# A grouped convolution moved between two parts of a linear layer's products on TensorE

## What is computed

```python
out = lax.conv_general_dilated(x, weight, ..., feature_group_count=4)   # 32 -> 32 channels, 9 taps
out = out + ctx[:, :, None] + bias[None, :, None]
base_out = einsum('btd,od->bto', out, base_W) + base_b                  # 512 -> 512
logits = einsum('btd,nd->btn', out, router_W) + router_b                # 15 routes
topk_p, topk_i = top_k(softmax(logits), 8)
w = einsum('btk,btke->bte', topk_p, onehot(expert_map[topk_i]))         # weight of each of 8 experts
h = einsum('btd,erd->bter', out, A)                                     # 8 x 16 = 128 columns
lora = einsum('bter,eor->bto', h * w[..., None], B) * 2.0
x + base_out + lora
```

## Time and profile before

| | us |
|---|---|
| median of three runs | 198.47 (196.33 to 198.89) |
| the profiled execution | 197.38 |
| its span, first to last instruction | 195.6 |
| TensorE busy | 187.3 |
| VectorE busy | 161.1 |
| GpSimd busy | 139.1 |

### The profile page before, as it was taken

One profiled execution on the slowest core, in us unless ns is written; L12 is line 12 of the kernel. 1 busy time (PEld: TensorE's weight loads), 2 busy tenths in 40 slices (PEclk: granted clock), 3 DMA queues, 4 the chain that ended last, 5 costly groups with the idle time before them and its releaser, 6 DMA issues.

```text
span 195.6 us, 4329 instructions
## 1 busy us (share of the span) xinstructions
PE 187.3 (96%) x1297; PEld 180.1 (92%) x1297; DVE 161.1 (82%) x547; ACT 76.9 (39%) x197; POOL 139.1 (71%) x115
## 2 busy tenths in 40 slices
PE   7899699999999999999999999999999999998993
PEld 2788599999999999999999999999999999997992
DVE  0899987888889888889888889888898889775663
ACT  3674434434333444433334444343344443122210
POOL 4539796777887777777887777778877777943520
PEclk9999969999999999999999999999999999999999
DMA  5985442455444434445443335444334133333312
GB/s 180 312 292 214 111 140 80 159 167 162 146 124 124 152 116 153 162 162 157 125 140 123 134 130 162 162 162 147 137 110 150 71 86 111 107 107 109 111 54 107
DMA packets 19051, 27.66 MB, mean 141 GB/s; under 512 B 2144, under 2 KB 9696, under 8 KB 19040
## 3 DMA queue, kind: packets, MB, share of 16 engines
q1 hardware_dynamic: 18576, 27.05, 42.6%
q10 hardware_dynamic: 432, 0.48, 0.7%
q0 software_dynamic: 32, 0.01, 0.2%
HBM read 19.14 MB, written 8.39 MB: 141 GB/s over the span
## 4 chain that ended last, share of the span: by engine, by line
PE 83%; DVE 8%; DMA 4%; issue 2%; ACT 1%; DVEq 0%; ACTq 0%
PE wide_ps L516 53%; PE conv_banks L498 15%; PE wide_ps L540 10%; DMA wide_sb<-wide_w 2%; DMA x_in<-x_first 2%; PE hwt_bank L527 2%; PE conv_banks L516 1%; DVE terms L672 1%; DVE y_rows L647 1%; DVE xr L642 1%; DVE wide_lo L757 1%; DVE y L731 1%; DVE spread L703 0%; DVE expert_w L707 0%; ACT wide_hi L324 0%
## 5 line engine op out<-in xcount | busy, mean ns | idle before, releaser
L516 PE MATMUL wide_ps<-wide_hi,y_hi 128*128 128x400 f32 (+1 forms) x248 | 80.4, 329 | 1.1 <-DVE xr L642 0.8
L516 PE MATMUL wide_ps<-wide_lo,y_hi 128*128 128x400 f32 (+1 forms) x248 | 77.1, 315 | 0.0
L516 PE MATMUL wide_ps<-wide_hi,y_lo 128*128 128x400 f32 (+1 forms) x248 | 76.8, 314 | 0.0
L437 POOL TENSOR_TENSOR terms_lo<-terms,terms_hi 128x768 fp32r<-128x768 f32 x28 | 51.6, 1842 | 31.8 <-ACT terms_hi L345 31.8
L516 PEld LDWEIGHTS wide_ps<-wide_hi,y_hi 128*128 128x128 f32 x248 | 46.6, 189 | 3.5 <-issue 1.0
L516 PEld LDWEIGHTS wide_ps<-wide_lo,y_hi 128*128 128x128 f32 x248 | 46.9, 190 | 0.0
L516 PEld LDWEIGHTS wide_ps<-wide_hi,y_lo 128*128 128x128 f32 x248 | 46.6, 189 | 0.0
L432 POOL TENSOR_TENSOR xr<-xr,biases_sb 128x512 f32<-128x512 f32 x32 | 41.3, 1291 | 5.6 <-DMA xr<-x_rows 5.5
L443 POOL TENSOR_TENSOR y_lo<-y,y_hi 128x512 fp32r<-128x512 f32 x31 | 40.2, 1295 | 3.3 <-ACT y_hi L352 3.3
L359 ACT ACTIVATE hw_hi<-hwt_bank 128x128 fp32r<-128x128 f32 x31 | 8.6, 277 | 81.7 <-PE hwt_bank L527 81.7
L352 ACT ACTIVATE y_hi<-y 128x512 fp32r<-128x512 f32 x32 | 20.2, 632 | 17.9 <-PE wide_ps L516 16.8
(11 more groups left out here) (93 smaller groups left out, 256.3 us busy)
## 6 DMA issues: line engine op xcount, KB each, us to landing
xr<-x_rows SPq DMA_DIRECT2D x32, 256.0 KB, 2.7
out<-xr SPq DMA_DIRECT2D x31, 256.0 KB, 2.0
even<-x_even SPq DMA_DIRECT2D x28, 132.0 KB, 2.6
terms<-x_odd SPq DMA_DIRECT2D x28, 128.0 KB, 2.8
wide_sb<-wide_w SPq DMA_DIRECT2D x4, 328.0 KB, 5.1
x_in<-x_first SPq DMA_DIRECT2D x2, 260.0 KB, 4.3
x_in<-x_pair SPq DMA_DIRECT2D x1, 520.0 KB, 5.9
biases_sb<-biases SPq DMA_DIRECT2D x1, 263.5 KB, 4.3
```

Source lines behind the costliest of these rows:

```text
L437: nc.gpsimd.tensor_tensor(terms_lo[i % 2][:, :, :, :], terms[i][:, :, :, :], terms_hi[i % 2][:, :, :, :].bitcast(F32), ALU.subtract)\
L516: mm = nc.tensor.matmul(sums_of(t, k)[:, b, 0:columns[1] - columns[0]], a[k % 2][:, r, :], w[:, r, columns[0]:columns[1]], start=r == 0 an ...
```

## The change

In each step from 1 to 27, the nine matmuls of `conv(t)` go from the end of the step to the place behind `turn_hw(t - 1)`, ahead of the remaining linear products. No instruction is added or taken away, and no wait is edited.

```diff
                     turn_hw(t - 1, k - 1)
+                    if up_to_tile(t, TILES - 5):
+                        conv(t, k, p)
                     linear(t, k, runs[:3], (NEXT_BANK,))
                     up(t - 1, k - 1)
                     linear(t, k, runs[3:], (NEXT_BANK,)).then_inc(linear_done, 1)
-                if from_tile(t, 1) and up_to_tile(t, TILES - 5):
-                    conv(t, k, p)
```

## The result

The changed kernel takes 218.78 us in the median of four runs (217.32 to 219.04), where the kernel before, run beside it, took 197.40 (196.25 to 198.89). The ratio is 1.106 with a 95% interval of 1.096 to 1.117: slower by about 11%. The profiled execution took 219.04 us, against 197.38: 21.66 us more.

What follows compares the result with a forecast made beforehand. The prediction took TensorE's own issue, 5.54 us a step, to bound the kernel. It summed 197.38 us (profiled execution), 21.1 us for 26 boundaries and 1.0 us for step 1 to 219.5 us, range 214 to 225.

Steps and rivals of the forecast that it cites:

- The boundary: Between steps, behind steps 2 to 27: the front waits for uncovered `add_out`, 0.81 us lost at each of 26, 21.1 us.
- What comes last: Ahead of `add_out`: VectorE is free at 4.65 of a step, `up` lets it start at 5.45, so `up` comes last.
- Step 1: In step 1 the moved convolution waits for GpSimd's `terms_lo` and the clock may fall: 1.0 us more, between -0.1 and 1.5.
- the first rival: At every boundary the clock falls, 1.61 us each, 41.9 us more: 261 us; chance 5%.
- the rows of step 29: In the kernel before, behind the single 0.85 us wait at step 29, the granted clock stayed at 1.00 for 7.5 us.
- VectorE did not stay last: Rival, at every boundary: `choose` late by 0.8 us or more keeps VectorE last, 1.07 us each, 226.7 us; chance 4%.
- `add_out` was not covered: Rival, at the boundaries: the three matmuls behind `up` cover `add_out`, no boundary costs anything, 194.0 to 197.4 us; chance 4%.

Runs made afterwards that it cites:

- the run with `up` behind the convolution: Against the changed kernel: step 1's convolution back at its end; in steps 2 to 27 `up` directly follows the early convolution, ahead of remaining linear products; 196.57 us, ratio 0.997.
- the run with step 1 as before: Against the changed kernel: unit 1's convolution stays at the end of step 1, so it moves in steps 2 to 27 only; 218.36 us, ratio 1.106.
- three early: Against the changed kernel: only the convolution's first three matmuls go early, six stay at the step's end behind `up`, step 1's convolution at its end; 198.15 us, ratio 1.006.

## Why the prediction was right

The forecast was 219.5 us in a range of 214 to 225; measured were 218.78, and 219.04 in the profiled execution.

*The boundary.* Forecast 0.81 us lost at each of 26, measured 6.316 - 5.542 = 0.774, so 20.1 us in place of 21.1. The links were read from single rows and hold: 0.51 us from `up` to `add_out` in both, 0.68 forecast and 0.69 measured for `add_out`, 0.15 to the front in both. The mis-sized part is small: the 0.05 us for the slower start behind a wait are there (0.26 us to the second matmul), but the rest of the step is a little shorter than I counted, 2.71 us from the transpose to the last pair of `up` where I had 1.66 + 1.07 = 2.73, and the step of 5.52 us from whose rows I worked is 0.02 shorter than the mean step of 5.542 from which the loss is measured.

*What comes last.* The count that gave VectorE 0.8 us of reserve (free at 4.65, `up` at 5.45) is confirmed by 0.71 us of idle time ahead of `add_out`, and from the other side by the run with `up` behind the convolution, where the reserve is gone and `add_out` starts directly behind the weighing: counted from a front's start at 104.47 - 5.54 = 98.93, that is 103.58 - 98.93 = 4.65. Had I priced the boundaries by the one that was in the trace, 1.07 us behind step 28, they would have come to 27.8 us where 20.1 were lost: that boundary had the same wait, but another cause.

*Step 1.* Forecast 1.0 us with bounds of -0.1 and 1.5; measured 10.77 - 9.39 = 1.38, with a fall of the clock in both, and 9.26 - 9.39 = -0.13 where it did not fall in the changed order. Without a fall in either, it is 9.26 - 8.49 = 0.77: step 1 then loses as much as any other boundary. But one working figure in it was wrong: I held that the slow clock cost the kernel before 1.61 us in this step. Step 1 in the same order and without a fall takes 8.49 us (the run with step 1 as before), so it cost 9.39 - 8.49 = 0.9. The runs with three early, which have that same step 1, agree: two with a mean clock of 0.99 took 198.98 and 198.99 us, four with 1.00 took 197.94 to 198.19. The rest lay under a wait that comes without a fall: in that run the front waits 0.51 us for VectorE's `add_out`, and from the convolution to the front it takes 1.73 us in both (28.33 - 26.60 there, 27.08 - 25.35 before). In the sum the figure only set the upper bound. In the changed order, where TensorE's own work sets the time from the convolution to `up`, the fall cost 1.51 us, so the first rival's price is not refuted by this.

*The rivals.* The clock did not fall at the boundaries: 1.00 over 164 us with a wait of 0.58 us every 6.3 us, as the rows of step 29 had pointed to. VectorE did not stay last (0.71 us idle). `add_out` was not covered, as three matmuls behind `up` are too few: with six more of them there, 0.065 us a step were still lost.

The remaining 21.66 - 20.1 - 1.4 = 0.2 us lie ahead of the transpose of step 1 (20.98 against 20.85) and behind that of step 28. That the forecast hits the profiled execution to half a us is partly luck: the boundaries were 1.0 us too high, and step 1 and the rest 0.6 too low.

## What to carry to other kernels

Before moving work on the engine that bounds a kernel, look at what it stands between: work behind a producer (`up`) and ahead of a wait for the consumer of its result (`add_out`) is cover, and moving it costs the uncovered part of that chain at every turn, even if the moved work gets no longer. Price the new wait link by link from rows where the same link is the last one, not from a place where the same wait has another cause. And if something must go early, move the producer with it: with `up` behind the convolution the same move was free.

## What was not expected of the hardware

The start of single executions differs by 1.7 us ahead of any step that the edits touch. In five of the ten profiled executions the transpose of step 1 comes at 20.57 to 20.98 us, in the other five at 22.12 to 22.26. In the run with step 1 as before, one of the late ones, the first groups of four convolution matmuls look like this in the timeline, and the window around them like the row below:

```profile
5.90 1.22 PE L476 MATMUL wide_ps<-x_hi,conv_hi 128*128 128x256 f32 x4 [0.55 <-ACT x_hi L318]
6.92 1.05 PE L476 MATMUL wide_ps<-x_hi,conv_lo 128*128 128x256 f32 x4
7.77 1.05 PE L562 MATMUL odd_bank<-cond_in_sb,cond_w_sb 128*128 128x128 f32 x4
```

```profile
5.90:9.48 3.58, 3.58 (x16) 3.58 (x17) 2.02 (x4) 2.07 (x4) 2.60 (x5) 1.00 1.00 281
```

In the run with three early, one of the others, the same rows are these:

```profile
5.99 0.75 PE L476 MATMUL wide_ps<-x_hi,conv_hi 128*128 128x256 f32 x4 [0.65 <-ACT x_hi L318]
6.58 0.64 PE L476 MATMUL wide_ps<-x_hi,conv_lo 128*128 128x256 f32 x4
7.06 0.61 PE L564 MATMUL odd_bank<-cond_in_sb,cond_w_sb 128*128 128x128 f32 x4
```

The second group of four takes 7.77 - 6.92 = 0.85 us to the next group, 0.21 us a matmul, in the one and 7.06 - 6.58 = 0.48, 0.12 a matmul, in the other: the two spacings of step 1 of the changed kernel, at 0.51 and at 1.00. The 1.00 in the window's row does not speak against that. The trace's record of the granted clock begins at 10.04 us in the late execution and at 5.53 in the other, and the window counts as 1.00 what lies ahead of it. So the late starts are matmuls at the lower level, up to about 10 us. In both executions TensorE had run the same nine matmuls on zeros before, from 1.32 us on. Why the clock rises later in some executions than in others stays open.

Together with the fall in step 1, which comes in some executions and not in others, this is about as large as the spread of the runs of one kernel, so differences of 1% between these kernels had to be read from the traces, step by step, and not from the times.
